# A three-stage language-model tower on one core: steps 0 and 1 of its software pipeline in a new order

## The reference

```python
h = layernorm(word_emb[ids] + pos_emb + type_emb[types]) * gamma + beta
a = layernorm(h)
k, q, v = a @ Wk, a @ Wq, a @ Wv              # heads of 16
k, q = layernorm_per_head(k), layernorm_per_head(q)
dot = where(causal, q @ k.T / 4, -inf)         # per head, 128 x 128
h = h + (softmax(dot) @ v) @ Wo + bo
f = layernorm(h)
scores = softmax(f @ gate_w.T); sel = top_k(scores + expert_bias, 2)
h = h + sum over the 2 chosen of silu(s*f @ w1[e]) * (s*f @ w3[e]) @ w2[e]   # s: its score
```

## Time and profile before

| | us |
|---|---|
| median of 3 runs | 553.78 (553.62 to 554.09) |
| the profiled execution's own time | 553.11 |
| its span in the trace | 551.4 |
| TensorE busy | 513.1 (93%) |
| VectorE, ScalarE, GpSimd busy | 288.8, 258.4, 271.6 |
| mean granted clock of TensorE | 0.987 of full |

### The profile page before, as it was taken

How to read it: one execution, slowest core, us unless ns; L and a number is a source line. 1 busy time by engine, 2 the same in 40 slices (tenths; PEclk the granted TensorE clock), 3 DMA queues, 4 the chain that set the end, 5 groups by cost and what they waited for, 6 DMA issues and landing times.

```text
span 551.4 us, 12949 instructions
## 1 busy us (share of the span) xinstructions
PE 513.1 (93%) x4260; PEld 430.8 (78%) x4261; DVE 288.8 (52%) x769; ACT 258.4 (47%) x591; POOL 271.6 (49%) x506
## 2 busy tenths in 40 slices
PE   6788999999999889789999999999999999999991
PEld 2345767777676666389999999999999999999980
DVE  3786888878888897723333333333333333333330
ACT  1068888988999784142333233322333223332320
POOL 4587787677754311214344543454434544444432
PEclk9899999999999999899999999999999999999997
DMA  5017611100028674211222212221122212222231
GB/s 164 10 39 273 211 50 42 46 29 29 29 74 274 213 229 122 57 31 23 38 39 39 29 29 39 39 39 24 34 39 39 33 27 37 39 37 30 30 39 20
DMA packets 29482, 36.64 MB, mean 66 GB/s; under 512 B 7792, under 2 KB 23024, under 8 KB 29456
## 3 DMA queue, kind: packets, MB, share of 16 engines
q0 software_dynamic: 8352, 12.76, 13.6%
q1 hardware_dynamic: 20288, 22.51, 12.8%
q10 hardware_dynamic: 816, 1.06, 0.5%
HBM read 26.81 MB, written 9.50 MB: 66 GB/s over the span
## 4 chain that ended last, share of the span: by engine, by line
PE 78%; DVE 5%; POOL 4%; DMA 3%; ACT 3%; issue 3%; ACTq 0%; DVEq 0%; POOLq 0%
PE PS L1369 35%; PE PS L1380 18%; PE PS L1107 9%; PE PS L1219 6%; DMA x_pair<-word_dram,idx 2%; PE PS L1195 2%; PE PS L1321 2%; PE PS L1178 2%; PE PS L1170 2%; PE PS L1115 1%; ACT work L602 1%; PE PS L1232 1%; DMA out_dram<-x_pair,dst_c 1%; DVE w_sb L825 1%; POOL arena L462 1%
## 5 line engine op out<-in xcount | busy, mean ns | idle before, releaser
L1369 PEld LDWEIGHTS PS<-work,arena 128*128 128x128 f32 x1716 | 197.6, 192 | 3.9 <-ACT work L706 2.0
L1369 PE MATMUL PS<-work,arena 128*128 128x128 f32 x1716 | 198.1, 275 | 1.5 <-ACT work L706 1.5
L712 ACT ACTIVATE work<-PS 128x768 f32<-128x768 f32 x39 | 31.6, 811 | 197.2 <-PE PS L1369 197.2
L1380 PE MATMUL PS<-w_sb,work 128*128 x468 | 107.6, 379 | 0.7 <-DVE x_pair L1082 0.7
L1074 DVE TENSOR_TENSOR work<-work,PS 128x640 f32<-128x640 f32 x39 | 32.0, 821 | 139.6 <-ACT work L712 139.6
L1380 PEld LDWEIGHTS PS<-w_sb,work 128*128 128x128 f32 x468 | 85.9, 190 | 11.2 <-issue 1.1
L549 POOL DMA_INDIRECT out_dram<-x_pair,dst_c x39 | 79.9, 2049 | 21.9 <-POOL dst_c L548 20.5
L602 ACT ACTIVATE work<-PS,nmax 128x128 f32<-128x128 f32 x256 | 73.0, 407 | 6.2 <-DVE nmax L836 6.2
L548 POOL COPY dst_c<-dest_i 128x1 int32 (+1 forms) x39 | 7.1, 183 | 137.2 <-DVE x_pair L1082 134.7
L702 ACT ACTIVATE arena<-w_sb 128x1408 f32 x40 | 55.1, 1377 | 13.8 <-DVE er_i L1050 8.9
L1107 PE MATMUL PS<-ident,work 128*128 128x128 f32 x336 | 55.3, 278 | 1.6 <-ACT work L602 1.4
(11 more groups left out here) (162 smaller groups left out, 612.9 us busy)
## 6 DMA issues: line engine op xcount, KB each, us to landing
w_sb<-w_dram SPq DMA_DIRECT2D x16, 640.0 KB, 6.2
w_sb<-w_dram SPq DMA_DIRECT2D x8, 704.0 KB, 4.6
x_rows<-x SPq DMA_DIRECT2D x16, 128.0 KB, 1.9
out_dram<-arena SPq DMA_DIRECT2D x16, 128.0 KB, 2.1
w_sb<-w_dram SPq DMA_DIRECT2D x16, 64.0 KB, 6.5
w_sb<-w_qkv_dram ACTq DMA_DIRECT2D x1, 768.0 KB, 8.1
work<-x_rows,src_c POOLq DMA_INDIRECT x41, 2.9
out_dram<-x_pair,dst_c POOLq DMA_INDIRECT x39, 4.2
```

The source lines that it names most:

```text
L1369: last = n.matmul(up_ps[p][:, i, c, :], ws[p][:, k, at:at + P], xT_sb[p][:, k, :], start=(k == 0), stop=(k == DK - 1))
L1380: last = n.matmul(PS[:, 7, 0:D], hT_sb[p][:, i, :], w2_sb[:, bass.ds(e, 1), i, :], start=(i == 0), stop=(i == FK - 1))
```

## The change

It moves code in steps 0 and 1 and changes two counts of warm-up matmuls: 42 instead of 32 at the very start, 7 instead of 14 in step 0. The work on tiles is the same.

```diff
-WARM_START, WARM_FIRST, WARM_EXPERTS = 32, 14, 16
+WARM_START, WARM_FIRST, WARM_EXPERTS = 42, 14, 16
...
 # GpSimd, step
                     if valid(t + 5):
                         gather(t + 5, 1 - p, link)
+                    if at_step(t, 0):
+                        qk_power(2, link)
                     if valid(t + 4):
                         power_e(t + 4)
-                    if valid(t + 2):
+                    if valid(t + 2) and not at_step(t, 0):
                         qk_power(t + 2, link)
...
 # ScalarE, step, after the copy of a_n's transposes
+                if at_step(t, 0):
+                    for r in range(RG):
+                        exponentials(r)
+                    transposed(0)
+                    transposed(1)
+                    queries_and_keys_out(1)
+                    transposed(2)
+                    squares(2)
+                    values_out(1)
+                    transposed(3)
+                    return
...
 # VectorE, step
                 elif at_step(t, -1):
                     normalize_a(2)
                     squared_sums(1)
-                    sum_rows(3, 1, 1)
-                    centered(3, 1)
                 if valid(t):
                     maxima(0)
                     maxima(1)
                     maxima(2)
                     maxima(3)
                 if at_step(t, 0):
+                    sum_rows(3, 1, 1)
                     normalize_qk(1)
+                    centered(3, 1)
                     first_norm(3)
                     stats(link, row(3), 1, var_a)
...
+                if at_step(t, 1):
+                    normalize_qk(2)
                 if valid(t + 4) and valid(t):
                     sum_rows(t + 4, p, half(4))
+                if at_step(t, 0):
+                    squared_sums(2)
...
-                if valid(t + 2) and valid(t):
+                if valid(t + 2) and valid(t) and not at_step(t, 0):
                     squared_sums(t + 2)
...
-                if valid(t + 2) and valid(t):
+                if valid(t + 2) and valid(t) and not at_step(t, 0):
                     normalize_qk(t + 2)
...
 # TensorE, step
                 if valid(t):
                     scores()
-                if at_step(t, 0):
-                    keep_warm(WARM_FIRST, T_BANK)
...
                     transposes(a_n, DK, O_BANK).then_inc(aT_ps, 1)
+                if at_step(t, 0):
+                    keep_warm(WARM_FIRST // 2, T_BANK)
+                    keys_to_rows(0)
+                    keys_to_rows(1)
+                    keys_to_rows(2)
+                if at_step(t, 1):
+                    outputs(0)
...
                     transposes(qkn, 2 * DK, T_BANK).then_inc(qk_ps, 1)
-                if valid(t - 1):
+                if valid(t - 1) and not at_step(t, 1):
                     outputs(t - 1)
```

More of the change, by code:

```diff
@@ L1280, in step @@
                     project(u, aT[p], QK_BANK, 0, 2 * D, qk_done)
-                if valid(t):
+                if valid(t) and not at_step(t, 0):
                     keys_to_rows(0)
@@ L1289, in step @@
                     outputs_back(t - 1)
-                if valid(t) and not at_step(t, B - 1):
+                if valid(t) and not at_step(t, 0) and not at_step(t, B - 1):
                     keys_to_rows(1)
```

## The result

The changed kernel takes 555.08 us (median of 12 runs), before 553.36 (12 runs): a ratio of 1.0035, 95% interval 1.0019 to 1.0051. That is 1.7 us by the medians and 1.9 by the ratio. Its profiled execution took 555.35 us, a span of 553.6, where that of before had 551.4.

The account below looks back on a forecast made before the run. TensorE's matmul chain was taken to bound steps 5 to 14, and GpSimd's queue to end last into step 1. 553.11 + 1.8 (start's -0.75 inside) = 554.9, plus 0.67 for the median: 555.6 us, range 554.2 to 557.3.

Parts of the forecast that it names:

- The new wait: Into step 1, VectorE's first_norm(4) waits more than 4 us, until about 45.2, for GpSimd's power_e(4), now behind qk_power(2).
- The start: Prologue: ten more start matmuls keep the clock up, project(0) ends at about 20.2, not 20.98: -0.75 us; otherwise +0.7.
- Step 0's gain: End of step 0: scores(1) can start near 40 instead of 43.70, 3.7 us earlier.
- What is late next: Step 1: project(3) starts at 50.3, not 47.99, +2.3 us; end of step 1 +1.6 to +2.3, taken as +1.8.
- the first rival: Step 1: the clock falls to half and isn't back before project(3): +1.2 us, 556.8 us; chance 0.22.
- The second rival: Step 1's idle time and the routing's clock fall give up to 1.7 us back: 554.0 us; chance 0.18.
- the third: Into step 1: first_norm(4) finds its root in time, VectorE isn't held, project(3) comes earlier: 551.4 us; chance 0.10.

Follow-up runs that it names:

- the pair at full clock: Two variants of the changed kernel with TensorE's idle pieces filled by warm matmuls: GpSimd's order kept, 554.41 us (ratio 1.0035), or undone, 551.54 us (0.9968).
- the first experiment: The changed kernel with GpSimd's order of before in step 0, power_e(4) ahead of qk_power(2): 553.55 us where before is 552.99, ratio 1.0017.

## Why the prediction was right

Forecast were 555.6 us, 1.8 more than before; measured 555.08, 1.7 more by the medians of 12 runs, of which that of before is 553.36 and not the 553.78 of three. The new wait and its way to `project(3)` were as forecast. That the size fits is in part luck: `project(3)` was less late than forecast, and the clock, which the sum left out, made up for it.

*The start.* Forecast: the clock kept up, -0.75. Right in mechanism, too small: the squares of tile 0 start at 19.86 instead of 21.02 (1.16), and 42 matmuls alone give 1.07 of the whole. The term missed that `project(0)` starts only 0.20 later, not 0.7: the matmuls take the place of an idle piece of 1.34 us, and they are done at 17.06, not 17.5. It isn't certain either: in one profiled execution with 42 (the product ahead of the maxima) they were done at 16.12, 1.37 us were idle behind them and the clock fell all the same; in one with 32 (GpSimd's order alone) it didn't.

*Step 0's gain and the new wait.* Forecast: `scores(1)` near 40, VectorE held for more than 4 us until 45.2, maxima of step 1 at 46.6, `normalize_qk(2)` at 49.0. Measured: 39.37, 4.01 us until 44.25, 45.67, 48.07. From the first norm on all are 0.9 early against the forecast, of which 0.4 is the start's gain, about 0.3 that the ten operations took 3.21 us (40.14 to 43.35) and not 3.49, and 0.2 that the issue of the gather took 1.07 and not 1.31. VectorE did not go around the wait: the scores for its maxima had been there since 40.5. The cause is shown by its removal (idle 0.81 us, `project(3)` 3.1 earlier), by the swap alone (+0.49%) and by the pair at full clock (3.3 us).

*What is late next.* Forecast: `project(3)` at 50.3, +2.3, and +1.8 at the end, inside +1.6 to +2.3. Measured: 49.71, +1.72; scores of step 2 +1.53, a little under the lower bound, but those of step 5 +2.10, and 1.7 to 1.9 in the timed runs. The forecast closed 0.5 us of the delay within step 1; what reached the later steps was not less than the delay of `project(3)` but more, and by the way that the forecast named as the other one, through `qk_power(3)`. It starts at 55.12 instead of 52.72, `normalize_qk(3)` is 2.38 late, and TensorE, early by then, waits 0.48 us for it. The chain of waits shows what `qk_power(3)` is late by: `project(3)`, the transposes of the attention output, VectorE's division and squared sums:

```profile
49.92 2.47 PE PS L1236 x4
...
53.30 0.27 DVE rden L980
...
55.12 0.42 POOL nwt L435
...
59.43 0.66 PE PS L1124 x4
```

*The clock.* The forecast had the clock back before `project(3)`, and gave the opposite 0.22. That step was wrong: it was at half from 44.5 to 51.3, `project(3)` took 2.68 us (1.98 in the earlier trace rows), `outputs(0)` 1.94. So the first rival's mechanism was there, with 0.7 us in `project(3)` where 1.2 was priced. (By the forecast's own numbers, half of a stretch of 3.4 us at half clock, that price would have been 0.85; and its count of two falls in the trace of before leaves out a third, from 543.8 to the end.) These 0.7 us stand on the chain above: 1.72 late at the start of `project(3)` and 0.70 from its length make the 2.4 by which everything behind it is late. By the same sum, a `project(3)` at 50.3 with this clock would have brought 3.0; the 0.6 us by which it came before the forecast hid most of the missing term. The second rival (the delay is made good) is refuted by steps 2 to 5, and the fall in the routing came again (232.2 to 235.6); the third (VectorE isn't held) is refuted by the 4.01 us. The forecast calls that one closed by the order of VectorE's queue; that order alone doesn't close it, since it turned on when GpSimd makes the root.

What stays open: how much of the half clock the changed kernel pays in the median, 0.7 us being that of one execution. Filling its gap alone gave no gain that can be told from none. At a like mean granted clock the difference between the kernels is all there, though: the changed kernel's eleven runs at 0.984 or 0.985 have a median of 555.02 us, before's eleven at 0.985 (those timed with the first experiment) 552.81, the first experiment's five at 0.985 or 0.986 552.67. These were timed at different times and a mean clock doesn't say where it was lost, so the 2.2 us are an estimate. The falls change their place from one execution to the next (at 18, 35, 44 or 46 us, and in eight of the eleven traces once more in the routing, between 226 and 238), so that profiles of single executions don't add up to the medians.

## What to carry to other kernels

In a pipeline with one queue for each engine, look at what a moved block of work delays on its own engine, and who waits for that. Against the first experiment, ten small operations ahead of two smaller ones made their own result 1.16 us earlier (43.35 to 44.51) and held the engine that waits for the other by 3.10 (44.25 to 41.15); the product that reads the early result stood behind it, and so did all that the change had won. And when a wait goes away, check the length of the matmuls behind it: here 1.3 us of a gain of 3.1 in starts went to the half clock, and thirteen matmuls that compute nothing got it back.

## What the runs showed of the hardware

The clock fell without any long idle piece: in the first experiment behind pieces of 1.49 and 0.56 us, with two transposes between and `outputs(0)` behind, while 2.43 us without one instruction passed without a fall in the earlier trace rows, and pieces of 1.50 and 0.56 us at the same place with both moves back. The same instructions don't always give the same clock: the changed kernel and the one with its gap filled are the same up to the scores of step 1, and only the second fell, at 35.0. One kernel's time also differed from run to run: with GpSimd's order undone, six runs with a mean granted clock of 0.985 to 0.988 took 552.49 to 552.78 us, the six with 0.981 or 0.982 took 554.33 to 554.99. Two microseconds between these groups of one kernel, as much as the change itself, go with the clock; that the clock is their cause is likely but not shown. The Trainium skill, page "TensorE: Matmul & The Clock Gate", section "What's actually happening", says that the point at which the clock first rises varies from run to run with where the first matmul falls; the traces agree, as the 42 start matmuls took from 10.63 us (42 alone) to 12.05 (the gap filled), and they show more, since the later falls move too.
